# q's second chunk ahead of the transpose of x and of gate and up, in the order of three engines

## What is computed

```
q = relu(x @ Wq).reshape(b, s, 64, 64) / 8
k = relu(x @ Wk).reshape(b, s, 64, 64)
v = (x @ Wv).reshape(b, s, 64, 64)
kv  = einsum('bsid,bsjd->bsdj', k, v)
out = einsum('bsid,bsdj->bsij', q, kv)
out = out / (einsum('bsid,bsd->bsi', q, k.sum(axis=2)) + 1e-6)
x = layernorm(x + out.reshape(b, s, 4096) @ Wo + bo)
gate, up = fp4_linear(x, w_gate), fp4_linear(x, w_up)      # 128 -> 352
h = silu(gate) * up
x = layernorm(x + fp4_linear(h, w_down))                   # 352 -> 128
```

## Time and profile before

| | |
|---|---|
| median of 3 runs | 2271.95 us (2269.57 to 2275.17) |
| the profiled execution | 2271.46 us |
| its span, first to last instruction | 2269.7 us |
| granted TensorE clock, mean of the span | 0.985 of full speed |
| busy: PE, PEld | 2050.3 us (90%), 1961.0 us (86%) |
| busy: DVE, POOL, ACT | 1805.8 us (80%), 1690.7 us (74%), 1618.7 us (71%) |
| chain of work that ended last | PE 55%, POOL 18%, issue 9%, ACT 9%, DVE 6%, DMA 2% |

### The profile page before, as it was taken

One profiled execution on the slowest core, in us unless ns is written; L12 is line 12 of the kernel. 1 busy time (PEld: TensorE's weight loads), 2 busy tenths in 40 slices (PEclk: granted clock), 3 DMA queues, 4 the chain that ended last, 5 costly groups with the idle time before them and its releaser, 6 DMA issues.

```text
span 2269.7 us, 88816 instructions
## 1 busy us (share of the span) xinstructions
PE 2050.3 (90%) x37963; PEld 1961.0 (86%) x37963; DVE 1805.8 (80%) x3359; ACT 1618.7 (71%) x3210; POOL 1690.7 (74%) x2192
## 2 busy tenths in 40 slices
PE   4799999999999999999999999999999999999975
PEld 3788998898898898898899899899899889889874
DVE  6778888888888888888888887888888888888873
ACT  4667777777777777777777777777777777777761
POOL 4577787787787787787787778778778778778772
PEclk9999999999999999999999999999999999999996
DMA  6467656666656666756756766765765665665661
GB/s 194 95 133 151 139 127 146 141 130 142 148 125 139 147 132 134 156 126 133 159 124 134 153 132 129 155 133 127 152 137 127 148 141 127 143 146 126 139 130 33
DMA packets 523216, 308.32 MB, mean 136 GB/s; under 512 B 275590, under 2 KB 497734, under 8 KB 522310
## 3 DMA queue, kind: packets, MB, share of 16 engines
q1 hardware_dynamic: 522822, 302.65, 61.9%
HBM read 17.38 MB, written 4.19 MB: 10 GB/s over the span
## 4 chain that ended last, share of the span: by engine, by line
PE 55%; POOL 18%; issue 9%; ACT 9%; DVE 6%; DMA 2%; SPq 0%; DVEq 0%; ACTq 0%; POOLq 0%
PE ps L408 15%; PE ps L361 12%; PE ps L363 12%; PE ps L362 12%; POOL o_st L1078 8%; POOL q_nat L1068 7%; ACT q_bd L564 6%; DVE q L798 3%; PE ps L434 3%; DVE o L816 2%; ACT hqT L571 2%; POOL small L1086 2%; PE ps L445 1%; DMA x_in<-in_L_attn_x 1%; ACT ks L577 1%
## 5 line engine op out<-in xcount | busy, mean ns | idle before, releaser
L1078 POOL TENSOR_TENSOR o_st<-o,o_st 128x256 bf16<-128x256 f32 x1024 | 659.8, 679 | 5.9 <-ACT o_st L639 5.9
L1068 POOL TENSOR_TENSOR q_nat<-q,q_nat 128x512 bf16<-128x512 f32 x512 | 590.3, 1176 | 33.2 <-ACT q_nat L597 32.9
L639 ACT CAST o_st<-o 128x256 bf16<-128x256 f32 x1024 | 358.4, 403 | 214.8 <-DVE o L816 211.0
L361 PE MATMUL ps<-v_st,q_bd 128*128 128x66 bf16 x4096 | 456.3, 198 | 42.9 <-DVE o L816 37.5
L361 PEld LDWEIGHTS ps<-v_st,q_bd 128*128 128x128 bf16 x4096 | 419.7, 114 | 61.9 <-DVE o L816 56.3
L362 PE MATMUL ps<-v_st,q_bd 128*128 128x66 bf16 x4096 | 454.0, 198 | 0.0
L363 PE MATMUL ps<-v_st,q_bd 128*128 128x66 bf16 x4096 | 452.5, 197 | 0.0
L816 DVE TENSOR_TENSOR o<-ps,rec 128x512 f32<-128x512 f32 x512 | 344.5, 683 | 120.7 <-POOL o_st L1078 110.2
L362 PEld LDWEIGHTS ps<-v_st,q_bd 128*128 128x128 bf16 x4096 | 417.5, 116 | 0.2 <-issue 0.2
L363 PEld LDWEIGHTS ps<-v_st,q_bd 128*128 128x128 bf16 x4096 | 416.8, 115 | 0.0
L408 PE MATMUL ps<-w_o,o_st 128*128 128x128 bf16 x6144 | 376.9, 220 | 3.4 <-DMA o_st<-swap 3.4
(11 more groups left out here) (129 smaller groups left out, 5334.4 us busy)
## 6 DMA issues: line engine op xcount, KB each, us to landing
q_bd<-q_nat SPq DMA_DIRECT2D x256, 256.0 KB, 3.9
swap<-v_st SPq DMA_DIRECT2D x64, 576.0 KB, 5.1
v_st<-v_st SPq DMA_DIRECT2D x64, 576.0 KB, 5.6
v_st<-swap SPq DMA_DIRECT2D x64, 576.0 KB, 5.4
swap<-o_st SPq DMA_DIRECT2D x64, 512.0 KB, 4.9
o_st<-o_st SPq DMA_DIRECT2D x64, 512.0 KB, 6.8
o_st<-swap SPq DMA_DIRECT2D x64, 512.0 KB, 5.5
x_in<-in_L_attn_x SPq DMA_DIRECT2D x64, 64.0 KB, 5.3
```

The source lines that it names most:

```text
L361: nc.tensor.matmul(dst, lhs(0), rhs(0), start=True, stop=False)
L639: last = nc.scalar.copy(ost[1 - t.par][:, 0, :, a, g * G:(g + 1) * G, :], src[:, a])
L1068: last = nc.gpsimd.tensor_tensor(qnat[:, 1, a, :, e, :], src[:, a], qnat[:, 0, a, :, e, :], ALU.subtract)
L1078: last = nc.gpsimd.tensor_tensor(lo[:, :, a], src[:, a], hi[:, :, a], ALU.subtract)
```

## The change

Three places, each a step moved within the list of one engine; no step is added, removed or altered. On PE q's second chunk comes ahead of xq's transpose and of gate and up. On ACT the conversion of q's first chunk comes ahead of the copy of xqT, and the conversion of the first out group ahead of the sigmoid. On DVE the scaling of q's second chunk comes ahead of `gate_sig` and `h_up`.

```diff
@@ PE, iteration @@
                 out_group(t, 0)
                 k_sum(t)
                 out_group(t, 1)
+                project(t, "q", 1)
                 xq_transpose(t)
                 gate_up(t)
-                project(t, "q", 1)
                 out_group(t, 2)
@@ ACT, iteration @@
                 x1_keep(t)
                 norm_o(t, 1)
+                q_hi(t, 0)
                 xq_copy(t)
-                q_hi(t, 0)
+                o_hi(t, 0)
                 sigmoid(t)
-                o_hi(t, 0)
                 o_hi(t, 1)
@@ DVE, iteration @@
                 scale_o(t, 0)
                 scale_o(t, 1)
+                q_scale(t, 1)
                 gate_sig(t)
                 h_up(t)
-                q_scale(t, 1)
                 h_max(t)
```

## The result

The changed kernel takes 2311.34 us, median of four runs (2308.91 to 2313.65), against 2270.95 before in the same comparison: the ratio is 1.0174, 95% interval 1.0158 to 1.0191. It is slower by 40 us, 1.7%; 2307 was forecast. The profiled executions differ by 2308.91 - 2271.46 = 37.5 us. The rest of the 40 lies in the spread of the runs, which goes with the clock: the runs of the changed kernel lie near 2309 at a mean granted clock of 0.984 and near 2313 at 0.980 to 0.981.

A forecast was written before the change was run, and what follows sets the result against it. PE was taken as nearly full, the period of 33.78 us set by a chain through q_scale(0) and GpSimd to out5. 0.52 plus 0.06 gives 0.58 a tile, times 61 is 35.4 us: 2307, range 2284 to 2329.

The forecast's parts named there:

- q1 waits for q_scale(0) and brings no cover for it: On PE, q1 shares PSUM slot 2 with q0 and waits for q_scale(0): new wait of 0.98 us in issue time.
- The wait for xqT moves along: On PE between transpose and gate: the wait stays, since the transpose moves together with gate_up; still about 0.5 us.
- VectorE's way, 0.52 at out5: Gate through sigmoid, gate_sig and h_max to scale_o(2), 0.85 us late; behind it out5 on PE is 0.52 late a tile.
- GpSimd, 0.06: GpSimd, 0.8 us late from q_lo(1), delays scale_o(7), v_hi(0) and v_lo(0), so v3 adds 0.06 a tile.
- The rule of the Trainium skill: Independent matmul groups should rotate through PSUM banks; alone it charges q1's whole exposed evacuation, 0.93 us a tile, giving 2328.
- nothing is absorbed: Rival: the whole lateness of scale_o(2) or out2 comes through, 0.85 to 0.95 us a tile, 2323 to 2329; chance 0.12.
- nearly all is absorbed: Rival: PE's slack takes nearly all the lateness, leaving 0.07 to 0.25 us a tile, 2276 to 2287; chance 0.10.
- Faster: Rival: scale_o(2) and scale_o(3) come earlier, closing the waits ahead of out4 and out5: 0.52 us a tile, 2240; chance 0.05.
- The order does not matter: Rival: instructions only change places inside existing waits and out5 stays bound by o_lo(1), 2265 to 2278; chance 0.03.

## Why the prediction was right

The sign, the size (2307 against 2311, range 2284 to 2329) and the mechanism held. Two rows that the steps below need are VectorE's v_lo(0) in the changed kernel, with two like instructions behind it (it takes 1.23 as in the earlier trace rows), and v0 on PE in the kernel before:

```profile
1166.06 3.67 DVE L781 TENSOR_TENSOR v_st<-ps,v_st 128x1024 bf16<-128x1024 f32 x3 [0.95 <-ACT v_st L540]
```

```profile
1145.20 0.22 PE L361 MATMUL ps<-xT,w_v 128*128 128x128 bf16 x1
```

By its steps:

- *q1 waits for q_scale(0) and brings no cover for it*: q1 started 0.06 after the release instead of 0.05; PE's new wait is 0.83 in this tile, 0.8 to 0.9 was said.
- *The wait for xqT moves along*: 0.45 instead of 0.5, still in every tile. With the transpose ahead of q1 it vanishes, and the loss with it: shown.
- *VectorE's way, 0.52 at out5*: 0.37. The links from q1 to h_max came within 0.05; the term was mis-sized at h_scale, 0.39 to the next instruction instead of 0.55. I had taken what it took in one row for its price, though that depends on GpSimd (last section).
- *GpSimd, 0.06*: 0.23 (0.28 by the run with q_hi(1) early). Its lateness, 0.79 at q_lo(1), was right, and so was the one link by which I let it come through: v_lo(0) ends at 1166.06 + 1.23 = 1167.29, 20.80 after q_scale(0), where 20.79 was forecast, and v3 starts just behind it. What I missed is an earlier link: scale_o(6) already waits 0.45 for o_lo(4) and ends at 1163.10, and v0 behind it starts 16.76 after q_scale(0) where it was 16.23 before, 0.53 late with out5 only 0.37 late. So the loss is 0.37 at out5, 0.16 more at v0 and 0.07 more at v3, together 0.60, where I had 0.52 and 0.06. That the mis-sized term and the missed link gave almost the same lateness at v0 is luck. But v3 waits for v_lo(0), and by these rows it would be 0.60 late at any smaller lateness of v0: the two ways don't add at v3, the later one decides. No run closes VectorE's way alone to show it.
- *The rule of the Trainium skill* ("Perfetto Trace Analysis", "Matmuls") gave 2328. In the run with the transpose ahead of q1, q1 starts as closely behind the release of its banks (0.06), and the loss is 2.3 us (at most 4.5 by the interval), so in this kernel the slack and the work inside the wait decide, not the rotation.
- The rival *nothing is absorbed* (0.85 to 0.95) and the rival *nearly all is absorbed* lay on either side; PE's waits for scale_o show the slack being spent, 40.2 to 19.5 us. *Faster* failed as it had to: scale_o(2) came later, not earlier. *The order does not matter* failed with out5, which moved by 0.37.

## What to carry to other kernels

Do not put a step that waits ahead of the first half of a round trip (transpose, copy on another engine, use): with the first half ahead of the wait, the wait covers the trip; here that is worth 37 of 40 us. Before moving a step forward ask which loop sets the period, and whether the step is on it; q1 was not. When an engine gets late, follow all the slots that it frees, the nearest first, and move the orders of the engines together: one engine's part of this move alone cost up to 138 us.

## What the runs showed of the hardware

*A small VectorE instruction held by GpSimd.* h_scale works on 22 numbers a partition and takes 0.64 us in the tile before, 0.42 after and 0.18 with VectorE's move alone. In the run with a copy on GpSimd the like instruction x_scale (L867 in that kernel), on 8 numbers, took 3.08 us; VectorE and GpSimd there:

```profile
1124.76 3.08 DVE L867 TENSOR_SCALAR xsc<-xsc 128x8 f32<-128x8 f32 x1
```

```profile
1124.22 3.60 POOL L1115 TENSOR_TENSOR q_bd<-q_nat,consts 64x2048 bf16<-64x2048 bf16 x1
```

It ends at 1127.84, GpSimd's copy at 1127.82; k_fold, k_sum and the whole loop stand behind it. Now h_scale in the tile before, with the first two of GpSimd's o_lo instructions:

```profile
1133.36 0.64 DVE L941 TENSOR_SCALAR hsc<-hsc 128x22 f32<-128x22 f32 x1
```

```profile
1132.66 1.30 POOL L1078 TENSOR_TENSOR o_st<-o,o_st 128x256 bf16<-128x256 f32 x2
```

h_scale ends at 1134.00, the second o_lo instruction at 1133.96; in 116 of the 122 full tiles of the kernel before and the changed one this distance is 0.03 to 0.04 us. So these instructions last as long as what GpSimd has under way when they start, 0.16 to 0.18 at least, and a change that shifts the two engines against each other changes that. The profile shows it as a longer duration and not as a wait, so no wait row names GpSimd. The Trainium skill, page "SBUF — State Buffer", section "Who interferes with whom", says that VectorE's second pair of SBUF ports is GpSimd's only one, that tensor_scalar can enter a mode that uses it, and that whoever issues first keeps the pair for the whole instruction; these rows agree, though none of them shows the mode. I did not try the instruction in another form.

*The clock behind a wait of 2.16 us.* After the wait of 2.16 us ahead of gate PE's granted clock fell to 0.50 in most tiles of one run and about half the tiles of another, while the waits of 1.08 us per tile in the kernel before leave it at 1.00. In the run with a copy on GpSimd it fell behind the wait of 2.52 us in every tile of the middle. What decides between the tiles stays open.
